# An attention loop's hand-written order: normalising, projecting queries and weighing in other places

## What is computed

```python
xn = _layernorm(x, ln1_g, ln1_b)
qkv = xn @ in_proj_w.T + in_proj_b
...
scores = jnp.einsum('bhqd,bhkd->bhqk', q, k) / np.sqrt(HD) + mask[None]
attn = jax.nn.softmax(scores, axis=-1)
o = jnp.einsum('bhqk,bhkd->bhqd', attn, v)
o = o.transpose(0, 2, 1, 3).reshape(b, s, e)
x = x + o @ out_w.T + out_b
xm = _layernorm(x, ln2_g, ln2_b)
mlp = jax.nn.relu(xm @ w1.T + b1) @ w2.T + b2
return x + mlp
```

## Time and profile before

| | |
|---|---|
| median of 3 runs | 1711.88 us (1706.98 to 1714.66) |
| the profiled execution | 1713.82 us |
| its span, first to last instruction | 1712.1 us |
| TensorE busy | 1262.9 us, 74% |
| VectorE busy | 1140.9 us, 67% |
| ScalarE busy | 965.3 us, 56% |
| GpSimd busy | 998.9 us, 58% |
| mean granted TensorE clock | 0.873 |

### The profile page before, as it was taken

How to read it: one execution, slowest core, us unless ns; L and a number is a source line. 1 busy time by engine, 2 the same in 40 slices (tenths; PEclk the granted TensorE clock), 3 DMA queues, 4 the chain that set the end, 5 groups by cost and what they waited for, 6 DMA issues and landing times. The chain is left out here.

```text
span 1712.1 us, 37950 instructions
## 1 busy us (share of the span) xinstructions
PE 1262.9 (74%) x11717; PEld 1039.7 (61%) x11717; DVE 1140.9 (67%) x3828; ACT 965.3 (56%) x2002; POOL 998.9 (58%) x1152
## 2 busy tenths in 40 slices
PE   4688888888888888887458878747766628888750
PEld 2456666666666666665357878735554518878750
DVE  5377777777777777776555555548888735656548
ACT  2487877777777777775144444336666524444420
POOL 4234567767667667666745555534888845555450
PEclk8599999998999999988678998969899859999985
DMA  7121011111111111110332222211222122222218
GB/s 201 53 66 41 33 43 52 47 52 52 44 49 50 48 54 53 46 37 22 127 85 78 78 76 72 74 54 52 78 83 79 45 80 73 75 76 82 73 55 288
DMA packets 100818, 120.94 MB, mean 71 GB/s; under 512 B 17944, under 2 KB 80720, under 8 KB 100368
## 3 DMA queue, kind: packets, MB, share of 16 engines
q1 hardware_dynamic: 69600, 75.85, 14.9%
q0 software_dynamic: 17280, 35.95, 6.2%
q10 hardware_dynamic: 13744, 6.75, 1.4%
HBM read 49.45 MB, written 44.46 MB: 55 GB/s over the span
## 5 line engine op out<-in xcount | busy, mean ns | idle before, releaser
L1096 DVE TENSOR_TENSOR ebuf<-score_banks,region 128x768 f32<-128x768 f32 x256 | 243.9, 953 | 150.2 <-PE score_banks L809 143.7
L1333 ACT ACTIVATE region<-ebuf 128x768 f32<-128x768 f32 x256 | 216.9, 847 | 38.9 <-DVE ebuf L1096 34.8
L1311 ACT CAST copied<-max_banks 128x768 bf16<-128x768 f32 x256 | 204.7, 800 | 58.8 <-PE max_banks L797 55.8
L1745 POOL DMA_INDIRECT choice_rows<-first_yo,first_xg x142 | 137.3, 967 | 130.3 <-DVE first_yo L1865 96.3
L1745 POOL DMA_INDIRECT choice_rows<-second_yo,second_xg x142 | 137.1, 965 | 126.5 <-DVE second_yo L1865 92.3
L2161 POOL DMA_INDIRECT expert_rows<-d_rows,z_d_index x128 | 130.0, 1016 | 39.2 <-issue 31.9
L1614 POOL DMA_INDIRECT expert_rows<-d_rows,a_d_index x128 | 135.8, 1061 | 27.0 <-issue 21.3
L1821 ACT ACTIVATE first_silu<-first_bgu,first_biases 128x256 f32<-128x256 f32 x142 | 63.3, 477 | 130.1 <-PE first_bgu L1774 50.9
L1821 ACT ACTIVATE second_silu<-second_bgu,second_biases 128x256 f32<-128x256 f32 x142 | 62.9, 477 | 129.6 <-issue 52.2
L774 PE MATMUL max_banks<-identb,region 128*128 128x128 bf16 x512 | 109.8, 236 | 18.9 <-ACT copied L1311 17.7
L1857 DVE SCALAR_TENSOR_TENSOR first_hT<-first_bgu,first_biases,first_silu 128x256 f32<-128x256 f32 x142 | 64.3, 478 | 81.3 <-ACT first_silu L1821 49.1
(11 more groups left out here) (333 smaller groups left out, 4487.7 us busy)
## 6 DMA issues: line engine op xcount, KB each, us to landing
region_r<-region_r SPq DMA_DIRECT2D x192, 128.0 KB
first_xg<-expert_rows SPq DMA_DIRECT2D x71, 132.0 KB
second_xg<-expert_rows SPq DMA_DIRECT2D x71, 132.0 KB
z_rows<-choice_rows SPq DMA_DIRECT2D x32, 256.0 KB
c_rows<-choice_rows SPq DMA_DIRECT2D x16, 512.0 KB
out<-xres ACTq DMA_DIRECT2D x16, 256.0 KB
choice_rows<-first_yo,first_xg POOLq DMA_INDIRECT x142
choice_rows<-second_yo,second_xg POOLq DMA_INDIRECT x142
```

The lines of the kernel that those rows point to most:

```text
L1096: nc.vector.tensor_tensor(ebuf[:, half_of_ebuf(c, j), :, :], score_banks[:, :, 0:BK], bias32[:, plain(j), :], ALU.add).then_inc(scores_fre ...
L1311: nc.scalar.copy(copied[:, 2 * j:2 * j + 2, :], max_banks[:, :, 0:BK]).then_inc(maxed_free, 1)
L1333: nc.scalar.activation(p32[:, j % 4, :, :], ebuf[:, half_of_ebuf(c, j), :, :], ACT.Exp).then_inc(exped, 1)
L1745: pool.indirect_dma_start(choice_dram, bass.IndirectOffsetOnAxis(ap=xg[:, i % G, t, E:E + 1].bitcast(I32), axis=0), yo[:, i % 4, t, :], No ...
```

## The change

Three calls stand elsewhere. On TensorE the third weighing of a portion goes ahead of `max_T`, and the projection of queries goes behind the eighth fill. On VectorE `normalise` goes ahead of `row_stats` and the fourth mask addition. Nothing is added or removed, and the orders of ScalarE, GpSimd and SyncE stay.

```diff
@@ TensorE, body
                 out_proj(b - 1)
+                weigh(b, n, 2)
                 max_T(b + 1, after)
+                fill(b, n, 7, b + 2, before, 2)
                 project_q(b + 3)
-                fill(b, n, 7, b + 2, before, 2)
-                weigh(b, n, 2)
                 mlp_down(b - 2, 0)
@@ VectorE, body
                 norm_moments(b + 3, n)
+                normalise(b - 1)
                 row_stats(b - 3)
                 add_mask(b, 3)
-                normalise(b - 1)
                 number(b - 5)
```

## The result

The changed kernel takes 1639.43 us in the median of 4 runs (1637.26 to 1648.57), the kernel before 1713.27 (4 runs): a ratio of 0.9584, 95% interval 0.9538 to 0.9630. That is 73.8 us less. The time was forecast as 1639, and the total is right. Of the sum's four terms the wait is right in size, the two of the clock are together 15 us too small, and the one for part two has the wrong sign; a later start of the loop, 5 us, was not in the sum at all.

What follows compares the result with a forecast made beforehand. No engine was saturated: a ring of waits around TensorE bound the portion, the longest at L920. 49.5 + 27.5 + 2.5 - 6.5 = 73 us off 1711.9 gave 1639 us, with 8 in 10 between 1622 and 1668.

Steps and rivals of the forecast that it cites:

- the sum's four terms: Attention loop: 49.5 us for L920's wait, 27.5 for its clock falls, 2.5 for the TensorE moves, -6.5 for new falls.
- the two of the clock: TensorE's clock: 27.5 us won from 21 falls at L920 ending, 6.5 lost to falls behind new holes.
- part two: TensorE, third weighing ahead of max_T, project_q behind the last fill: 0.08 us won a portion, 2.5 us over 32.
- Part one, the wait: VectorE, normalise ahead of row_stats and add_mask(3): L920's wait goes from 1.69 to 0.09, 49.5 us in all.
- the some six falls: Clock falls put down to holes such as those at L763 and L745: most of 8 us, left in.
- the new holes of 1.10: Three TensorE waits, for copied maxima, last mask and last exponential, 0.36, 0.24 and 0.50; charged 6.5 us for falls.
- The rival that the clock keeps falling: TensorE: new holes, 1.10 in all, bring falls as often as the old wait; 1660 us, chance 0.22.
- The bound of 0.3 for the maxima's transfer: Part two's worst case: a transfer of 3.65 us holds the scores, losing 0.3 per portion, 10 us.
- VectorE did not eat half: Rival at L920: the mask addition's cover is lost and half the wait returns; 1673 us, chance 0.08.
- the signs named beforehand: Trace signs: L920's wait under 0.2, portions 20.2 to 20.7, L908 under 310 ns, VectorE's score wait down some 40 us.
- The slower case: Rival: the query chain carries both moved pieces, take_q 1.2 later, each portion losing 1.59; 1722 us, chance 0.05.
- Part one does nothing: Rival at L920: turning ends after VectorE is ready, so moving normalise wins nothing; 1711 us, chance 0.03.

Runs made afterwards that it cites:

- norm_only: The kernel before with only the VectorE edit, normalise ahead of row_stats and the fourth mask addition: 1490.92 us against 1574.27 on the same chip, ratio 0.9459.
- tensor_only: The kernel before with only the TensorE edit, third weighing ahead of max_T and project_q behind the eighth fill: 1577.02 us against 1574.27, ratio 1.0007.
- copy_first: The changed kernel with add_mask(b, 7) ahead of take_q and copy_for_max ahead of take_upper_q: 1610.41 us; the kernel before took 1718.85 on that chip.
- filled_wait: The kernel before with 20 added products that nobody reads in TensorE's wait at L920: 1539.20 us against 1574.27 on the same chip, ratio 0.9767.

## Why the prediction held, term by term

**Part one, the wait: right.** 1.60 per portion was forecast (wait from 1.69 to 0.09), 1.59 measured with it alone, and in the steady portions L920 has no wait that the trace would note, but for one of 0.2. That the delayed mask addition is covered held too: between 140 and 700 us norm_only's trace has a single wait of scores for the mask (0.8 us). At 1.59 the 30 portions give 47.7 of the 48.

**The clock: mechanism right, size wrong.** The sum had 27.5 - 6.5 = 21 us; about 36 came, nearly the whole loss. The count behind the 27.5 was nearly right: 21 falls at L920 were worked out from L908's mean, the record of the clock has 23, and the some six falls that it put elsewhere are 5 behind the holes and 1 at the end. The step that failed is that these were left in as independent of the wait (8 us) and that the new holes of 1.10 were charged as many again (6.5 us). They were not independent: in the kernel before every fall behind the holes came in a portion that had fallen at L920, and norm_only has the holes and none of these falls. The changed kernel has the new holes and a single fall in 29 portions, where every kernel has one. The rival that the clock keeps falling rested on the same step and is refuted by L908's 280 ns. The rule of the Trainium skill (TensorE: Matmul & The Clock Gate, "A second HAM failure mode: psum-queue depth-cycling"), that short idle times can keep the clock changing, fits this loop as long as it has the wait of 1.68; the three waits of 0.28 to 0.42 that remain do not do it here.

**Part two: wrong sign.** Forecast +2.5 us, measured 0.19 x 31 = 6 us lost. The step is the time at which the projection reaches ScalarE. The prediction took 0.65 from L745's start to `take_upper_q`, for which no row stood. The trace of after, where ScalarE waits for the projection, has 343.09 - 342.29 = 0.80. Before, it was 318.78 - 317.97 = 0.81: `take_upper_q` did start directly behind an exponential, as the prediction has it, but the projection was there only just then, so that any delay of it counts. So `take_q`, counted from the seventh fill's scores at 339.48, goes at 4.11 instead of 319.27 - 315.65 = 3.62, 0.49 later and not 0.26, and the weighing behind the next fill 0.16 later and not 0.08 sooner. The places of all new waits were right. The bound of 0.3 for the maxima's transfer did not come up: no wait for it is in the trace. An early reading was off as well: the 0.65 before L763 stands in a portion with two falls of the clock, while the even portion at full clock waited 0.33 there (294.87).

**Not in the sum: the start.** L920 first runs at 126.83 instead of 121.75, 5.1 us late, in a stretch at half clock (windows of after and of before):

```profile
117.80:124.60 6.80, 6.47 (x60) 4.69 (x52) 4.44 (x8) 4.59 (x9) 4.02 (x6) 0.50 0.07 22
```
```profile
117.80:124.60 6.80, 4.86 (x38) 4.22 (x39) 3.39 (x10) 3.99 (x7) 3.45 (x6) 0.82 0.23 82
```

In the other trace of the same kernel, after_again, it is 123.83, so part of it varies from run to run. tensor_only, with part two alone, starts latest of all, at 129.3, norm_only at 120.6; but copy_first, which holds part two as well, starts at 118.4. Whether part two delays the start was not settled.

**The balance.** The 29 portions of filled_wait and of norm_only, each from its first L920, stand between those of before and after:

```profile
123.31:762.12 638.81, 581.39 (x7446) 444.35 (x7446) 508.54 (x1423) 503.45 (x880) 449.25 (x562) 0.99 0.14 48
120.61:711.57 590.96, 542.94 (x6866) 410.29 (x6866) 505.00 (x1421) 503.57 (x881) 449.96 (x564) 0.99 0.15 52
```

Before to after is 675.67 - 595.76 = 79.9: 36.9 from before to filled_wait, which is the clock; 47.9 from there to norm_only, which is the wait (29 x 1.59 = 46.1) and the last two falls behind the holes; and 4.8 lost from norm_only to after, which is part two. Less 5.1 at the start, and with 0.9 and 1.8 after the last portion and in the later stages, the span falls by 77.5, from 1712.1 to 1634.6, where the sum had 73. The medians differ by 73.8. That the total hit to a microsecond is luck in the terms: about 15 us more from the clock than forecast, against 8.5 less from part two and 5.1 lost at the start, and medians that fell less than the profiled spans.

**The rivals.** VectorE did not eat half: the cover held. Of the signs named beforehand all came but two sizes: VectorE's wait for scores fell by 90 and not 40, and the odd portion at 20.84 is above the 20.2 to 20.7 that were given, by the loss of part two. The slower case needed `take_q` 1.2 later; it is 0.49 later. "Part one does nothing" is refuted by norm_only.

## What to carry to other kernels

A wait of under 2 us on TensorE in every pass can cost nearly as much again in clock as in waiting (1.23 on 1.59 here): look at the granted clock right behind the wait, and price it from passes at full clock. Filling the idle time with products that nobody reads tells the two apart in one run. Falls seen behind smaller holes need not be theirs: here they went with the long wait. When a piece of work is moved behind another, ask which order was only there for the sake of the old place; the gain here lay in moving the last mask addition and the copy of maxima along with it (30 us), while the move alone cost 6.

## What had not been expected

The falls behind the holes at L763 and L745 need the holes and some of the wait: taking away either ends them (none in tensor_only, none in norm_only, five before). The third weighing ahead of the maxima costs 0.1 us a portion in the changed kernel and wins 0.40 once the chain through `take_q` is cut. And adding 1240 instructions to the kernel before (620 products and their weight loads), with nothing else changed, makes it 35.1 us faster: 0.9767, 0.9727 to 0.9808.
